# First layer: gathering the own rows of a tile one tile ahead of the shared rows

## The reference

```python
def L0(features, adj, Wq, Wk):
    Qn = cos_normalize(features @ Wq.T)
    Kn = cos_normalize(features @ Wk.T)
    att = softmax(where(adj > 0, Kn @ Qn.T, -9e15), axis=1)
    prop = att @ features            # a row without neighbours keeps its features
    return 0.5 * prop + 0.5 * features

def L1(h, adj, W, b_W, a_vec, b_a):
    h = h @ W.T + b_W
    e = (h @ a1)[:, None] + (h @ a2)[None, :] + b_a
    return softmax(where(adj > 0, leaky_relu(e, 0.2), -9e15), axis=1) @ h

h = relu(layernorm(x));  x = x + L0(h, adj, Wq, Wk)
h = relu(layernorm(x));  x = x + L1(h, adj, W, b_W, a_vec, b_a)
```

## Time and profile before

| | |
|---|---|
| Median of 3 runs (lowest to highest) | 1582.53 us (1582.44 to 1582.91) |
| The profiled execution | 1582.28 us |
| Its span, first to last instruction | 1580.3 us, 21879 instructions |
| PE, PEld busy | 1084.1, 815.3 us |
| DVE, ACT, POOL busy | 1142.5, 964.1, 1078.5 us |
| q1 (SyncE): packets, MB | 49128, 277.05 |
| q0 (GpSimd's gathers): packets, MB | 34304, 71.42 |
| Mean granted TensorE clock | 0.838 of full speed |

### The profile page before, as it was taken

The page is one execution under the profiler, slowest core; times in us unless marked ns, Lnnn a source line. Parts: engine busy times, 40 slices in busy tenths (PEclk is TensorE's granted clock), DMA queues, the critical chain, the costliest instruction groups (busy, mean ns, idle before and its releaser), DMA issues.

```text
span 1580.3 us, 21879 instructions
## 1 busy us (share of the span) xinstructions
PE 1084.1 (69%) x5729; PEld 815.3 (52%) x5729; DVE 1142.5 (72%) x4489; ACT 964.1 (61%) x2795; POOL 1078.5 (68%) x1121
## 2 busy tenths in 40 slices
PE   6977777788867877877775456556555665555556
PEld 4653545555555555554565335445444554445445
DVE  6995698879887888888776256566666676656666
ACT  5663867778778777877678644454445444544423
POOL 2246777677776767776676377777777777777774
PEclk9997899989999988999888666787788777777777
DMA  9999999999999999999942122222222222222221
GB/s 361 421 388 390 374 399 400 403 347 400 398 394 365 399 399 377 399 398 402 395 169 53 44 55 61 61 60 61 58 61 60 61 59 60 61 60 60 59 60 41
DMA packets 90474, 358.45 MB, mean 227 GB/s; under 512 B 23653, under 2 KB 36328, under 8 KB 57576
## 3 DMA queue, kind: packets, MB, share of 16 engines
q1 hardware_dynamic: 49128, 277.05, 44.1%
q0 software_dynamic: 34304, 71.42, 17.2%
q10 hardware_dynamic: 6912, 8.52, 1.5%
HBM read 344.18 MB, written 12.72 MB: 226 GB/s over the span
## 4 chain that ended last, share of the span: by engine, by line
POOL 36%; DMA 27%; issue 14%; PE 11%; DVE 6%; ACT 5%; SPq 0%; ACTq 0%; POOLq 0%; DVEq 0%
DMA arena<-in_adj_dram 25%; POOL arena L542 19%; POOL arena L537 13%; PE ps L1029 5%; POOL arena L967 3%; DMA arena<-tab,idx_shared 2%; PE ps L1052 2%; POOL arena L975 2%; ACT prod L1217 2%; PE ps L1064 1%; PE ps L1066 1%; DVE norm L1381 1%; ACT R L1187 1%; ACT R L1185 1%; PE ps L1010 1%
## 5 line engine op out<-in xcount | busy, mean ns | idle before, releaser
L967 POOL DMA_INDIRECT arena<-tab,idx_own x320 | 322.2, 1007 | 128.5 <-issue 92.4
L542 POOL DMA_INDIRECT arena<-tab,idx_own x320 | 303.0, 947 | 97.5 <-issue 97.5
L1029 PE MATMUL ps<-arena,fold 128*128 128x512 fp8e4 x1024 | 285.8, 414 | 108.4 <-DMA arena<-in_adj_dram 108.2
L607 ACT ACTIVATE arena<-arena,negm 128x773 f32<-128x773 f32 (+1 forms) x64 | 58.5, 914 | 362.8 <-DVE negm L681 362.8
L975 POOL DMA_INDIRECT arena<-tab,idx_shared x216 | 210.5, 974 | 93.3 <-issue 57.5
L537 POOL DMA_INDIRECT arena<-tab,idx_shared x216 | 204.1, 945 | 87.4 <-issue 65.5
L557 PE MATMUL ps<-prod,column 128*128 128x384 f32 (+1 forms) x128 | 103.2, 905 | 231.2 <-DVE prod L633 231.2
L1029 PEld LDWEIGHTS ps<-arena,fold 128*128 128x128 bf16 x1024 | 91.7, 101 | 258.7 <-DMA arena<-in_adj_dram 153.5
L1217 ACT ACTIVATE prod<-prod,arena 128x128 f32<-128x128 f32 x528 | 203.4, 390 | 0.0
L633 DVE TENSOR_TENSOR prod<-ident,arena 128x384 f32<-128x384 f32 (+3 forms) x70 | 39.5, 571 | 220.7 <-DMA arena<-tab,idx_shared 220.7
L580 PEld LDWEIGHTS ps<-arena,diag 128*128 128x128 f32 x640 | 142.8, 315 | 45.6 <-issue 40.9
(11 more groups left out here) (202 smaller groups left out, 2496.7 us busy)
## 6 DMA issues: line engine op xcount, KB each, us to landing
arena<-in_adj_dram SPq DMA_DIRECT2D x256, 1024.0 KB
arena<-tab,idx_own POOLq DMA_INDIRECT x640, 2.7
arena<-tab,idx_shared POOLq DMA_INDIRECT x432, 2.6
tab<-arena ACTq DMA_DIRECT2D x16, 260.0 KB, 7.4
tab<-tw ACTq DMA_DIRECT2D x32, 130.0 KB
res<-in_x_dram SPq DMA_DIRECT2D x8, 512.0 KB, 11.8
out_dram<-arena SPq DMA_DIRECT2D x64, 64.0 KB, 1.7
prod<-in_L_gnn_Wq_dram SPq DMA_DIRECT2D x1, 64.0 KB
```

The lines of the kernel that those rows point to most:

```text
L542: pool.indirect_dma_start(out=GO[q][:, s, :], out_offset=None, in_=tab1, in_offset=bass.IndirectOffsetOnAxis(ap=idx_own[:, t, s:s + 1], ax ...
L607: nc.scalar.activation(sc[p][:, 0:K + n * P], sc[p][:, 0:K + n * P], ACT.Exp, bias=negm[:, p:p + 1]).then_inc(s_ex1, 1)
L967: pool.indirect_dma_start(out=G[t % GR][:, s, :], out_offset=None, in_=tab0, in_offset=bass.IndirectOffsetOnAxis(ap=idx_own[:, t, s:s + 1] ...
L1029: last = nc.tensor.matmul(keys_ps[t % 2], fold[:, PIECE_BITS * f + b, :], ring8[m % RING][:, b * WORDS:(b + 1) * WORDS], start=False, stop ...
```

## The change

In the first layer GpSimd's order becomes: own rows of tile 0; then for t = 1 to 63 the own rows of tile t, followed by the shared rows of tile t - 1; the shared rows of tile 63 at the end. The wait for the weighted sums stays ahead of the own rows, now for t from 5 to 63 in one loop; the number of buffers stays. The last tile's own rows, in two parts, now come ahead of the shared rows of tiles 62 and 63, and ScalarE, DVE and TensorE take the parts of the last tile in that order: own rows 0 to 2, own rows 3 to 4, shared rows.

```diff
--- before.py
+++ after.py
@@ -977,15 +977,17 @@
                             in_offset=bass.IndirectOffsetOnAxis(ap=idx_shared[:, t // QT, c:c + 1], axis=0),
                             bounds_check=None).then_inc(s_g[1][t % GR], 16)
 
-                for t in range(T - 1):
+                gather_own(0, 0, K, s_g[0][0])
+                for t in range(1, T):
                     if t >= GR:
                         pool.wait_ge(s_pv, t - GR + 1)
-                    gather_own(t, 0, K, s_g[0][t % GR])
-                    gather_shared(t)
-                pool.wait_ge(s_pv, T - GR)
+                    if t < T - 1:
+                        gather_own(t, 0, K, s_g[0][t % GR])
+                    else:
+                        gather_own(t, 0, 3, s_g[0][t % GR])
+                        gather_own(t, 3, K, s_last)
+                    gather_shared(t - 1)
                 gather_shared(T - 1)
-                gather_own(T - 1, 0, 3, s_g[0][(T - 1) % GR])
-                gather_own(T - 1, 3, K, s_last)
                 either(pool, lambda e: None, lists_gpsimd)
 
             @block.tensor
@@ -1069,16 +1071,16 @@
 
                 def weighted_last(t):
                     p, q, n = t % 2, t % GR, PAIRED[t % QT]
-                    pe.wait_ge(s_W, paired(t + 1))
                     pe.wait_ge(s_fin, t - 1)
-                    for j in range(n):
-                        v, s, e = shared(t, SPAN[t % QT][0] + j)
-                        nc.tensor.matmul(pv_ps[p][:, 0:ROW], W[p][j], Gc[:, e, :], start=j == 0, stop=False)
                     for part, (a, b) in enumerate(((0, 3), (3, K))):
                         pe.wait_ge(s_dg, t + 1 + part)
                         for s in range(a, b):
-                            last = nc.tensor.matmul(pv_ps[p][:, 0:ROW], diag[t % DR][:, s, :], G[q][:, s, :], start=False,
-                                                    stop=s == K - 1)
+                            nc.tensor.matmul(pv_ps[p][:, 0:ROW], diag[t % DR][:, s, :], G[q][:, s, :], start=s == 0,
+                                             stop=False)
+                    pe.wait_ge(s_W, paired(t + 1))
+                    for j in range(n):
+                        v, s, e = shared(t, SPAN[t % QT][0] + j)
+                        last = nc.tensor.matmul(pv_ps[p][:, 0:ROW], W[p][j], Gc[:, e, :], start=False, stop=j == n - 1)
                     last.then_inc(s_pv, 1)
 
                 def offsets_after(i):
@@ -1325,18 +1327,18 @@
                 weights(T - 2)
                 second.scalar_h(act, PAIRS - 4)
                 second.scalar_rows(act, PAIRS - 5)
-                last_scores(T - 1, K, slots(T - 1), 1)
-                last_exps(T - 1, K, slots(T - 1), 3, 1)
+                last_scores(T - 1, 0, 3, 1)
+                last_exps(T - 1, 0, 3, 3, 1)
+                last_diags(T - 1, 0, 3, 1)
                 second.scalar_root(act, PAIRS - 3)
                 second.scalar_hT(act, PAIRS - 4)
-                last_scores(T - 1, 0, 3, 2)
-                last_exps(T - 1, 0, 3, 6, 2)
-                last_diags(T - 1, 0, 3, 2)
+                last_scores(T - 1, 3, K, 2)
+                last_exps(T - 1, 3, K, K, 2)
+                last_diags(T - 1, 3, K, 2)
                 second.scalar_h(act, PAIRS - 3)
                 second.scalar_rows(act, PAIRS - 4)
-                last_scores(T - 1, 3, K, 3)
-                last_exps(T - 1, 3, K, 8, 3)
-                last_diags(T - 1, 3, K, 3)
+                last_scores(T - 1, K, slots(T - 1), 2 + len(runs(T - 1)))
+                last_exps(T - 1, K, slots(T - 1), slots(T - 1), 3)
                 second.scalar_hT(act, PAIRS - 3)
                 second.scalar_root(act, PAIRS - 2)
                 second.scalar_rows(act, PAIRS - 3)
@@ -1515,7 +1517,7 @@
 
                 def spill_weights(t):
                     p = t % 2
-                    dve.wait_ge(s_ex, t + 1)
+                    dve.wait_ge(s_ex, t + (3 if t == T - 1 else 1))
                     if t >= 2:
                         dve.wait_ge(s_pv, t - 1)
                     for j in range(PAIRED[t % QT]):
@@ -1622,12 +1624,12 @@
                 spill_weights(T - 3)
                 finish(T - 5)
                 dve.wait_ge(s_red, red(T - 2))
+                last_own_products(T - 1, 0, 3, s_g[0][(T - 1) % GR], go_before[(T - 1) % GR])
+                spill_weights(T - 2)
+                last_own_products(T - 1, 3, K, s_last, 32)
+                finish(T - 4)
                 spill_products(T - 1)
-                spill_weights(T - 2)
-                last_own_products(T - 1, 0, 3, s_g[0][(T - 1) % GR], go_before[(T - 1) % GR])
-                finish(T - 4)
                 second.vector_stats(dve, link, PAIRS - 3)
-                last_own_products(T - 1, 3, K, s_last, 32)
                 finish(T - 3)
                 spill_weights(T - 1)
                 finish(T - 2)
```

## The result

The kernel after takes 1808.88 us (median of 4 runs, 1806.6 to 1812.24) against 1582.72 us before (1582.44 to 1583.72): a ratio of 1.1433, 95% interval 1.1418 to 1.1447, so **slower by 226 us**. The forecast was 1802, with a range of 1690 to 1860. The profiled execution took 1807.51 us, its span is 1805.5.

A forecast was written before the change was run, and what follows sets the result against it. The adjacency stream on the DMA engines was taken to bound the first layer. To 1582.28 us were added 205.2 for the two-tile loop, 10 at the start and 4 at the end: 1802 us, range 1690 to 1860.

The forecast's parts named there:

- The ring: First-layer chain of waits from weighted sums t - 4 to t - 2: two tiles instead of three, 31.6 us, later 32.4.
- the sign of a wrong last link: TensorE waiting at L1024 for freed keys instead would mean the loop is right but its last link is not.
- The landing: Step term from the start of the last shared gather to DVE's multiply at L1513: 4.8 us.
- Rival 1: Stream pauses once TensorE sets the pace, so gathers land in 2.95 us: 1754 us; chance 0.15.
- L1037 (now L1039) to the end of the weighted sums: Step term on TensorE, from its wait for spill counts through folds and owner rows: taken 12.15 us.
- Rival 2: TensorE stays warm, so its stretch from the counts to the weighted sums stays at 8.7 us: 1733 us; chance 0.12.
- The two tiles between the parts: One tile of about 10 us between successive parts of the planner's tables, 20 us together.
- Last part: Weighted sums 40 to 56, decode and compact together behind extract: 8 steps of 32.4 us, less 2.2 once.
- The start: Up to tile 2, shared rows come five gathers later: +6 to +15 us, taken +10.
- The tail: End of the first layer, last tile reordered: -3 to +8 us, taken +4.
- Nothing moves: Shared rows' delay disappears in the stream's slack; only start and end count: 1580 to 1585 us; chance 0.03.
- faster: GpSimd's 26.2 us of waiting for indices filled with own gathers, at most that gained: 1556 us; chance 0.04.

The follow-up runs named there:

- old_four: Kernel before, old order, with four own-row buffers in place of five: 1790.45 us.
- six_own: Changed kernel with six own-row buffers in place of five, room made by a shared scratch tile: 1589.52 us.
- tail_only: Kernel before with only the last tile's part reordered as in the change: 1582.15 us.
- finish_early: Changed kernel with TensorE taking spill counts later, weighted sum ahead of the folds, and VectorE's finish(t - 5) ahead of tile t - 1's products: 1619.95 us.

## Why the prediction was right

**The ring.** It holds, link by link: freed buffer, own rows, shared rows, landing, products, counts, TensorE. The signs named were seen: DMA share 0.77 (about 0.75 forecast), TensorE's wait for the counts 265.1 us (over 100), GpSimd's wait for the buffer its largest, the wait for shared indices down from 26.2 to 10.7, the weighted sums of tile 56 ending 1052.7 - 829.14 = 223.6 us later (about 215), the second layer 1.1 us off. The granted clock fell to 0.80, as forecast below the 0.93 of before. old_four and six_own show that the two tiles in place of three are the cause. The keys at L1026, the sign of a wrong last link, waited 13.6 us in 3 places. But TensorE's counts are only the longest of several links from VectorE's step: cut there, the ring closes through the key bank, then through the bank of sums.

**Its size.** Tiles 2 to 56 took 842.6 us, against 839.2 worked out. That closeness is partly luck of terms that cancel, above all the first two; the means are over the steps of the changed kernel's trace:
- The landing was mis-sized. Taken 4.8 as a mean over busy and idle stream, with 5.4 for the busy one from a single landing, at which the DMA share was 0.72; measured 6.24 in the step shown, 6.08 in the median of those waited for, 5.7 in the mean of the 26 steps, which is 23 us more in all. A stream that is busy 0.77 of the time lengthens it as much as a full one, since it is full (0.94 or more in 21 of 24 landings) while the shared rows land. Rival 1 (2.95) falls: the landing was that short only in the few steps in which the stream paused, and halving the bytes brought it to 4.1. By the Trainium skill ("DMA: Bandwidth & Descriptors", section "Anatomy of one DMA — SWDGE (gpsimd) path") the estimate was 2.15; no landing in the ring's steps agrees, the shortest took 2.51.
- L1037 (now L1039) to the end of the weighted sums was mis-sized the other way: taken 12.15, measured 12.15 in the step shown (521.35 to 533.50), but 8.5 to 12.3 over the 18 steps up to tile 40 and 10.8 in the mean (the sum took 11.8 with its 6.6 off for folds), which is 18 us less in all. The granted clock was 0.50, so 1.2 GHz, for 3.5 us after a wait of 11.29 us, and 0.80 over the whole stretch. Rival 2 (8.7 throughout) falls, though a long wait does not always cost all that was taken.
- In the step shown, own gathers 6.25 (taken 6.57), product to counts 4.4 (4.6), each 0.2 to 0.3 too high; in the mean of the 26 steps the own gathers took 6.45.
- The two tiles between the parts: 9.0 and 15.6, taken 20 together.
- Last part, tiles 40 to 56: 261.8 us in 8 steps, 32.7 each, taken 32.4.

**The ends.** The start was taken as +10 and is +14.9, at the upper end of +6 to +15. About 5 of it the order costs with six buffers too (tile 2 ends at 200.6), with the hole in the stream. The tail was taken as +4 and is +0.5 in the changed kernel; tail_only shows none.

**The other rivals.** "Nothing moves" and "faster" hoped for slack, or for idle time of GpSimd to fill. The run six_own is the place where they could have been right, with the buffer that "ahead" needs: GpSimd still waits 27.6 us there for shared indices (26.2 before), and the time does not fall, because the stream bounds it.

## What to carry to other kernels

To issue a transfer earlier on an in-order queue pays no price in the steady loop only if its target is free then (six_own); with the same number of buffers the wait for the target comes ahead of everything behind it, and the loop of three tiles became one of two. Work out that loop from one turn of the chain, in us a tile, and compare it with the pace of what bounds the kernel: 10.8 against 11.7 hid it, 15.8 did not. When a ring has to be opened, look at the engine on which all ways back meet (here VectorE, whose whole step stands behind one wait), not only at the way back that the profile names as the longest.

## What was not expected

- Beside a stream that is idle a quarter of the time, gathers landed no sooner than beside a full one: 6.08 against 5.96 us in the median; at half the bytes (DMA share 0.60 from 240 to 629 us) it was 4.09. What counts is the share during the landing (0.99 in the one shown), not the mean over the stage (0.77).
- A reordering that needs no wait still cost 0.4%: a hole in the stream during 26 us of the start (0.83 against 1.00) is a loss for good when the stream bounds the rest. It makes about 4.4 of some 7 us. In finish_early, with the same order at the start, the share was 0.87 and tile 2 ended at 193.2, so the order alone does not fix the end of tile 2; the cause of the hole was left open.
- Three moves that take waits off TensorE's path made the kernel before slower by 0.33 to 0.62%, for a cause that no run here tells apart.
